# Two orders on GpSimd's queue changed in a fused expert-MLP and LoRA kernel: the adding transfer behind the next row's first sums, and C22 of step 10 ahead of the last pair's sums in row 0

## The reference

```python
# layer 0: a shared gelu MLP and the two routed experts of each row (E = 8, I = 1024)
def mlp(x, g, u, d):
    return (gelu(x @ g) * (x @ u)) @ d
w, sel = top_k(softmax(cond_8), 2)
w = w / w.sum(-1)
x = x + sum_e dense_w[:, e] * mlp(x, skill_gate[e], skill_up[e], skill_down[e]) \
      + mlp(x, shared_gate, shared_up, shared_down)
# layer 1: a linear map with a LoRA part that is weighted per row
x = x + (x @ W_base.T + b_base + 2 * lora(x, As, Bs, cond_8))
```

## Time and profile before

| | |
|---|---|
| median of 3 runs | 804.69 us (804.63 to 804.95) |
| the profiled execution | 805.2 us |
| its span | 803.5 us |
| PE busy | 790.1 us, 98% |
| DVE, ACT, POOL busy | 657.3, 498.6, 309.6 us |
| PE's granted clock | 0.999 |
| HBM traffic | 135 GB/s over the span |

### The profile page before, as it was taken

One profiled execution on the slowest core, in us unless ns is written; L12 is line 12 of the kernel. 1 busy time (PEld: TensorE's weight loads), 2 busy tenths in 40 slices (PEclk: granted clock), 3 DMA queues, 4 the chain that ended last, 5 costly groups with the idle time before them and its releaser, 6 DMA issues.

```text
span 803.5 us, 13795 instructions
## 1 busy us (share of the span) xinstructions
PE 790.1 (98%) x4277; PEld 686.5 (85%) x4277; DVE 657.3 (82%) x872; ACT 498.6 (62%) x808; POOL 309.6 (39%) x308
## 2 busy tenths in 40 slices
PE   9999999999999999999999999999999999999998
PEld 7888888888888888888889889888988888888897
DVE  4866888888887779978978987888888798789777
ACT  6554554654664566766767667576675667667673
POOL 1521321321330444345434453533644443454441
PEclk9999999999999999999999999999999999999999
DMA  7426506304816724654652565375356346543400
GB/s 204 124 74 198 143 1 200 116 0 144 258 43 185 249 79 105 217 152 106 202 163 87 137 226 132 77 235 159 92 159 214 95 104 222 144 105 102 118 17 28
DMA packets 139887, 108.76 MB, mean 135 GB/s; under 512 B 63040, under 2 KB 131392, under 8 KB 139840
## 3 DMA queue, kind: packets, MB, share of 16 engines
q1 hardware_dynamic: 138688, 104.00, 42.9%
q0 software_dynamic: 1152, 4.19, 3.1%
HBM read 83.53 MB, written 24.64 MB: 135 GB/s over the span
## 4 chain that ended last, share of the span: by engine, by line
PE 88%; DVE 6%; issue 3%; POOL 2%; ACT 1%; ACTq 0%; DVEq 0%; POOLq 0%
PE ps_ring L859 55%; PE ps_acc L859 32%; DVE post L1866 2%; DVE inner_lo L1589 1%; DVE post L1888 1%; DVE post L1903 1%; ACT ps_ring L1442 1%; POOL stage L804 1%; DVE wide L1589 0%; DVE xc L1589 0%; PE ps_ring L981 0%; POOL post L817 0%; PE ps_acc L1075 0%; PE ps_acc L975 0%; POOL stage L803 0%
## 5 line engine op out<-in xcount | busy, mean ns | idle before, releaser
L859 PE MATMUL ps_ring<-xc,wide 128*128 128x512 f32 (+1 forms) x1854 | 385.6, 356 | 0.0
L859 PEld LDWEIGHTS ps_ring<-xc,wide 128*128 128x128 f32 x1854 | 317.0, 189 | 52.9 <-DVE post L1651 0.9
L1204 ACT CAST inner_hi<-post 128x512 fp32r<-128x512 f32 x192 | 116.1, 621 | 103.9 <-DVE post L1979 28.4
L859 PE MATMUL ps_acc<-inner_hi,wide 128*128 128x512 f32 x504 | 166.3, 390 | 0.0
L1589 DVE TENSOR_TENSOR inner_lo<-post,inner_hi 128x512 fp32r<-128x512 f32 (+1 forms) x145 | 131.4, 915 | 3.9 <-ACT inner_hi L1204 3.5
L1207 ACT ACTIVATE post<-post 128x256 f32<-128x256 f32 (+1 forms) x114 | 62.1, 557 | 96.2 <-DVE post L1903 68.6
L817 POOL TENSOR_TENSOR post<-post 128x256 f32<-128x256 f32 x78 | 80.4, 1050 | 95.2 <-ACT post L1456 95.2
L859 PEld LDWEIGHTS ps_acc<-inner_hi,wide 128*128 128x128 f32 x504 | 94.8, 188 | 18.9
L859 PE MATMUL ps_acc<-inner_lo,wide 128*128 128x512 f32 x252 | 98.5, 391 | 0.0
L859 PE MATMUL ps_ring<-xc 128*128 128x256 f32 x576 | 79.9, 284 | 5.0 <-ACT ps_ring L1442 5.0
L859 PE MATMUL ps_acc<-inner_hi,sh_dn 128*128 128x512 f32 x256 | 83.9, 389 | 0.0
(11 more groups left out here) (127 smaller groups left out, 1070.6 us busy)
## 6 DMA issues: line engine op xcount, KB each, us to landing
rights_scratch<-xc SPq DMA_DIRECT2D x6, 1792.0 KB, 10.2
raw<-n_L_cond_skill_gate_dram SPq DMA_DIRECT2D x32, 256.0 KB, 2.9
raw<-in_L_cond_skill_up_dram SPq DMA_DIRECT2D x32, 256.0 KB, 3.4
raw<-n_L_cond_skill_down_dram SPq DMA_DIRECT2D x32, 256.0 KB, 4.0
xbuf<-n_L_cond_skill_gate_dram SPq DMA_DIRECT2D x32, 256.0 KB, 2.9
xbuf<-in_L_cond_skill_up_dram SPq DMA_DIRECT2D x32, 256.0 KB, 3.5
xbuf<-n_L_cond_skill_down_dram SPq DMA_DIRECT2D x32, 256.0 KB, 3.8
xt_scratch<-xbuf SPq DMA_DIRECT2D x8, 512.0 KB, 3.4
```

The source lines that it names most:

```text
L859: last = pe.matmul(dst, left_[a], right_[b], start=start and n == 0, stop=stop and n == len(PASSES) - 1, skip_group_check=adds)
L1204: return nc.scalar.copy(dst, src)
```

## The change

In POOL's `row`, two orders. In row 0, C22 of n_s = 2 (step 10) now comes ahead of the weights' sums of n_s = 4 (pair 7), not behind them. In rows 0 to 6 the first sums of the next row (n_s = 0 of row b + 1) now come ahead of `add_tokens(b)`. No instruction is added or removed, and nothing changes on the other engines.

```diff
                 sums_of_weights(b, 3)
-                sums_of_weights(b, 4)
-                ex_c22(b, 2)
+                if first:
+
+                    ex_c22(b, 2)
+                    sums_of_weights(b, 4)
+                else:
+                    sums_of_weights(b, 4)
+                    ex_c22(b, 2)
                 ex_c22(b, 3)
                 if not last:
+                    sums_of_weights(b + 1, 0)
                     add_tokens(b)
-                    sums_of_weights(b + 1, 0)
                 ex_c22(b, 4)
```

## The result

The changed kernel takes 794.63 us (median of 4 runs, 794.52 to 795.07) against 804.68 us before in the same comparison: a ratio of 0.9875 (95% interval 0.9858 to 0.9893), 10.05 us less. The forecast was 8.28 us less, 796.4 us, and its range began at 795.6. The direction and the mechanism held; the size of the main term, what a gap of PE costs, did not.

What follows compares the result with a forecast made beforehand. PE, busy 790.1 of 803.5 us, was taken to bound the kernel, so only filling its gaps pays. Gains of 6.6 + 1.53 + 0.15 = 8.28 us off 804.69 gave 796.4 us, range 795.6 to 799.0.

Steps and rivals of the forecast that it cites:

- The place and the cause of the gaps: PE's product n = 3, steps 12 and 14: 8.3 us waiting for ACT's copy; step 14's loss laid to transfer before sums.
- The prediction's reading of the overlap: POOL's sums behind a transfer: they overlap by 0.3 us, because of the transfer, and DVE finds no moment between them.
- What would be late next: Row 1, step 14: copy and product n = 6 each keep 0.6 us to spare; the transfer leaves 3.65 us later.
- Six rows give 6 x 1.10 = 6.6 us: Step 14 of rows 1 to 6: moving the transfer behind the sums regains each row's whole 1.10 us gap.
- The gain is 1.53: Step 14 of row 0: moving the transfer behind the sums removes PE's whole gap of 1.53 us.
- Nothing in it can bring much more, for it is nearly all of PE's gaps: Whole kernel: the forecast gain of 8.28 us takes nearly all of PE's gaps, 13.4 us in all.
- Part 2: Row 0, C22 of step 10 ahead of pair 7's sums: gains 0.15 us, 0.33 at best.
- The single train: POOL's sums hold the port together, transfer or not, so the multiply waits for S2: 798.0 us; chance 0.13.
- The transfer that holds DVE wherever it goes: Transfer's descriptor work holds DVE after the move too; PE waits 2.3 us at n = 6: 812.5 us; chance 0.06.
- Something else becomes late: Copy, L1888 or a later ACT or DVE step brings back about half of each gap: 800.4 us; chance 0.06.
- No effect: The 1.9 us DVE delay comes from something merely falling there, and PE waits as before: 804.5 us; chance 0.05.

Runs made afterwards that it cites:

- the settled run: Kernel before the change, with one tiny awaited POOL memset between the transfer and the next row's sums: 794.82 us, ratio 0.9877.
- the move to pair 7: Changed kernel, but in rows 1 to 6 the transfer goes directly in front of pair 7's S1, behind that S1's waits: 805.61 us, ratio 1.0011.
- the pair with 16 and 128 partitions: Changed kernel with a memset of 16 partitions, or of 128 as control, directly in front of the next row's sums: 800.35 us and 795.26 us.
- part 1 alone: Kernel before the change, with only the transfer moved behind the next row's sums in rows 0 to 6: 795.01 us, ratio 0.9876.
- part 2 alone: Kernel before the change, with only C22 of step 10 put first in row 0: 804.51 us, ratio 0.9996.

## Why the prediction was right or wrong

**The place and the cause of the gaps: right.** The chain PE, copy, cast, block-12 multiply, POOL's train was the one that counted, and the loss belonged to the transfer directly in front of the sums. It was argued from the earlier trace rows; the settled run, the move to pair 7 and the pair with 16 and 128 partitions show it. The prediction's reading of the overlap, that a transfer lets POOL's cores start unevenly, is supported by the last pair, where unevenness was made without a transfer. That a transfer does it by the same route was not seen directly: the trace does not show single cores.

The Trainium skill, page "SBUF — State Buffer", section "SBUF: two separate sides", gives the lock for one whole instruction; the trace agrees where neither a transfer nor the memset of 16 partitions stands directly in front (0.753 us behind S3) and not where one does, where DVE waited to the end of S2. The Trainium skill, page "GPSIMD Engine Reference", section "2.1 Instruction dispatch", has each core going on to the next instruction by itself; the runs with 16 and 128 partitions (1.72 and 1.02 us) agree with that.

**What would be late next: right.** The multiply was worked out to last about 0.75 us and lasted 0.753. The copy had 376.90 - 376.52 = 0.4 us to spare (0.6 was said, counted from the group's recorded end; from 379.42 it would have been 0.4), L1893 0.6 (377.77 + 0.69 against 379.05). The transfer left 3.42 us behind the sums' start (3.65 was said), and nobody waited for it.

**The sum: its main term was too small, and this is the step that failed.** "Six rows give 6 x 1.10 = 6.6 us" and "The gain is 1.53" took the idle time shown as the price of a gap. The traces show 1.35 a row and 1.72 in row 0: 6 x 1.35 + 1.72 = 9.82 instead of 8.13. The run of part 1 alone gained 9.88. The mistake is visible in rows that were there beforehand: the matmul group ahead ends 0.16 us later than the next one normally starts, and the group behind the gap is 0.09 longer. The prediction even used 2 x 0.72 in this way for n = 6 of row 0, and not for the gaps.

**The range: its lower end rested on the same mistake.** "Nothing in it can bring much more, for it is nearly all of PE's gaps" counted idle time as all that can be regained; 2.8 us of PE's "busy" time went too, about 1.7 of it at the seven gaps (9.82 less 8.13).

**Part 2: the size is not settled by the times.** 0.15 was said. By the trace, n = 0 to n = 6 of step 12 in row 0 went from 305.07 - 300.17 = 4.90 to 304.26 - 299.67 = 4.59, 0.31 less; n = 6 still waits, now for the split behind the sums, as predicted. The run of part 2 alone gained 0.38, with an interval that does not exclude zero.

**Span against median.** The span lost 10.6 us, the median 10.05. The profiled execution of before was 0.5 above its median, that of after at its median (794.57). The prediction had taken the 0.5 for both and forecast 796.9 for the second. In the traces these 0.5 us lie ahead of the change: the last product of row 0's step 10 starts at 296.70 before and 296.20 after. The gaps add up to 9.82 + 0.31 = 10.1.

**The rivals.** The single train (0.13) fell: the multiply got in behind S3. The transfer that holds DVE wherever it goes (0.06) fell with the changed kernel, where no gap stood at n = 6, and again in the settled run. "Something else becomes late" (0.06) did not show, but for the 0.08 us of row 0. No effect (0.05) fell.

## What to carry to other kernels

A PE gap in a timeline costs more than its idle time: compare the starts of the same two instructions in a disturbed and an undisturbed repeat. On GpSimd, keep a DMA issue, or an instruction on part of the partitions, away from a train of back-to-back instructions that DVE's two-SBUF-input operations meet; about 2 us between them, or one awaited tiny instruction, was enough here, though at pair 7 the awaited one put POOL's queue off and left the kernel 5.5 us over the changed one. And look for an instruction with two durations: the 2.347 against 0.474 us of one multiply led to the whole case.

## What the runs showed of the hardware

- A DVE operation that reads two tensors in SBUF and arrived during POOL's sums was kept out to the end of S2 if a transfer's issue (2.347 us instead of 0.474, arriving inside S1) or a 0.30 us memset of 16 partitions (1.72 us, arriving at S3's start) ran directly in front of them. With neither in front it got in behind the one running (0.753 us), and behind a memset of 128 partitions too (1.02 us).
- The transfer's issue by itself held nobody: the same multiply took 0.47 us at 0.97 us behind it.
- inner_lo, recorded 0.34 to 0.35 us behind the issue and 0.26 to 0.27 ahead of S1, once took 1.22 us and five times was held to S2's end: the recorded starts do not tell who gets in.
- A gap of PE cost more than the idle time shown: 1.35 us for 1.10, 1.80 for 1.53, 1.84 for 1.58.
